# State-space scan: the two differences of the three-part split of B and C on GpSimd instead of VectorE

## The reference, cut to what matters

```python
A = -jnp.exp(A_log)
x_dbl = jnp.einsum('bld,ed->ble', hidden_states, W_xproj)
dt_low = x_dbl[..., :DT_RANK]
Bm = x_dbl[..., DT_RANK:DT_RANK + D_STATE]
Cm = x_dbl[..., DT_RANK + D_STATE:]
delta = jax.nn.softplus(jnp.einsum('blr,dr->bld', dt_low, W_dt) + b_dt)
dA = jnp.exp(delta[..., None] * A)
dBx = (delta * x)[..., None] * Bm[:, :, None, :]
# per token: h = dA_t * h + dBx_t ; y = sum over n of h * C_t
```

## Time and profile before

| | |
|---|---|
| median of 3 runs | 1409.5 us (1409.46 to 1409.54) |
| the profiled execution | 1409.21 us, its span 1407.4 us |
| mean granted TensorE clock over the span | 0.928 |
| TensorE (matmul) busy | 1095.6 us, 78% |
| VectorE busy | 1001.4 us, 71% |
| ScalarE busy | 750.5 us, 53% |
| GpSimd busy | 792.1 us, 56% |

### The profile page before, as it was taken

One profiled execution on the slowest core, in us unless ns is written; L12 is line 12 of the kernel. 1 busy time (PEld: TensorE's weight loads), 2 busy tenths in 40 slices (PEclk: granted clock), 3 DMA queues, 4 the chain that ended last, 5 costly groups with the idle time before them and its releaser, 6 DMA issues. The chain is left out here.

```text
span 1407.4 us, 25930 instructions
## 1 busy us (share of the span) xinstructions
PE 1095.6 (78%) x8527; PEld 755.7 (54%) x8527; DVE 1001.4 (71%) x1898; ACT 750.5 (53%) x1601; POOL 792.1 (56%) x730
## 2 busy tenths in 40 slices
PE   5877778687777757888888888413999999999980
PEld 1332223232232326666666676302898999899970
DVE  2999999999999965777677677484455555555533
ACT  4667575666656624666556565202455555555433
POOL 2686776767777645666677666312234634463423
PEclk8999999999999988999999999556899999999995
DMA  3000000000000000111111110202234443443217
GB/s 106 16 15 1 16 0 15 1 15 15 0 0 0 1 21 13 40 41 34 34 34 34 35 40 25 83 0 93 69 60 111 89 101 73 112 87 73 41 22 252
DMA packets 43463, 64.01 MB, mean 45 GB/s; under 512 B 8288, under 2 KB 34592, under 8 KB 41248
## 3 DMA queue, kind: packets, MB, share of 16 engines
q1 hardware_dynamic: 31104, 46.11, 9.8%
q0 software_dynamic: 12288, 17.05, 7.5%
HBM read 42.00 MB, written 21.14 MB: 45 GB/s over the span
## 5 line engine op out<-in xcount | busy, mean ns | idle before, releaser
L514 POOL TENSOR_TENSOR scan_hc<-scan_state,scan_c_sb 128x1024 f32<-128x1024 f32 x128 | 304.4, 2383 | 143.0 <-DVE scan_state L442 133.6
L442 DVE TENSOR_TENSOR_SCAN scan_state<-scan_decay,scan_drive_ps 128x512 f32<-128x512 f32 x256 | 297.4, 1203 | 0.2
L223 PE MATMUL scan_y_ps<-scan_hc,all_ident 128*128 128x512 f32 x520 | 255.3, 614 | 2.1 <-POOL scan_hc L514 2.1
L1660 DVE TENSOR_TENSOR expert_hid_lo<-expert_hid,expert_hid_hi 128x512 fp32r<-128x512 f32 x128 | 88.6, 692 | 176.0 <-ACT expert_hid_hi L1644 176.0
L1557 POOL DMA_INDIRECT acc<-expert_rows,expert_lst x64 | 112.0, 1750 | 180.4 <-DVE expert_rows L1686 165.7
L1639 ACT ACTIVATE expert_hid<-expert_h_ps,expert_b 128x512 f32<-128x512 f32 x128 | 88.2, 689 | 199.2 <-PE expert_h_ps L556 199.2
L435 DVE TENSOR_TENSOR scan_drive_ps<-scan_dx,scan_b_ps 128x512 f32<-128x512 f32 x256 | 162.6, 681 | 14.9 <-POOL scan_dx L501 10.8
L326 ACT ACTIVATE scan_decay<-scan_delta,scan_a_neg 128x508 f32<-128x508 f32 x256 | 169.2, 715 | 7.4 <-POOL scan_delta L496 7.2
L368 ACT ACTIVATE scan_c_sb<-scan_c_ps 128x512 f32<-128x512 f32 x128 | 76.6, 598 | 138.0 <-PE scan_c_ps L216 128.9
L556 PE MATMUL expert_o_ps<-weights_w_hi,expert_hid_lo 128*128 128x256 f32 x512 | 143.3, 280 | 0.0
L554 PE MATMUL expert_o_ps<-weights_w_hi,expert_hid_hi 128*128 128x256 f32 x512 | 143.3, 280 | 0.0
(11 more groups left out here) (221 smaller groups left out, 2498.3 us busy)
## 6 DMA issues: line engine op xcount, KB each, us to landing
weights_w<-w SPq DMA_DIRECT2D x16, 1024.0 KB, 5.3
table<-all_row SPq DMA_DIRECT2D x32, 132.0 KB, 1.7
scan_xT<-xT SPq DMA_DIRECT2D x8, 512.0 KB, 3.9
attn_ctxT<-ctxT SPq DMA_DIRECT2D x32, 128.0 KB, 2.5
acc<-all_row SPq DMA_DIRECT2D x32, 128.0 KB, 1.7
final_a<-acc SPq DMA_DIRECT2D x8, 512.0 KB, 6.5
out<-final_o SPq DMA_DIRECT2D x8, 512.0 KB, 4.6
expert_b<-b SPq DMA_DIRECT2D x8, 128.0 KB, 2.9
```

Of the source, the lines that this page charges most:

```text
L223: last = pe.matmul(y_ps[k][:], ident[0][:], hc[:, n % RING, k, :], start=False, stop=(n == NS - 1))
L442: dve.tensor_tensor_scan(state[:, n % RING, k, :], decay[:, n % RING, k, :, :].rearrange("p b t -> p (b t)"), drive_ps[k][:], 0.0, ALU.mul ...
L514: pool.tensor_tensor(hc[:, n % RING, :, :], state[:, n % RING, :, :], c_sb[:, n % RING, :].unsqueeze(1).broadcast_to([P, KH, GT]), ALU.mul ...
L1660: dve.tensor_tensor(hid_lo[:, f % RING_H, :], hid[:, f % 2, :], hid_hi[:, f % RING_H, :].bitcast(F32), ALU.subtract).then_inc(hid_ready, 1)
```

## The change

Both differences go to GpSimd, and since it reads SBUF, ScalarE makes one more copy of the value, in f32, for it (`bc_full`, 64 rows). The parts stand in the opposite order: the last part in rows 0 to 31 of `bcs`, the middle in 32 to 63, the high part stays in 64 to 95. `bc_rest` has 64 rows instead of 96. ScalarE's middle part moves from behind step 9 to behind step 10, ahead of the softplus. TensorE's `step_size` waits for the copy (`bc_copied`) instead of for the difference, and the first broadcast of a group waits on `bc_step` instead of on `bcs_ready`.

```diff
@@ TensorE
                     pe.wait_ge(dt_copied, g + 1)
-                    pe.wait_ge(bc_high, g + 1)
-                    pe.wait_ge(bc_step, 4 * g + 1)
+                    pe.wait_ge(bc_copied, g + 1)
...
-                        pe.wait_ge(bcs_ready, g + 1)
+                        pe.wait_ge(bc_step, 4 * (g + 1))
@@ ScalarE
                     act.activation(bcs[par][:], m_ps[1][0:96, :], ACT.Copy).then_inc(bc_high, 1)
+                    if not first:
+                        act.wait_ge(bc_step, 4 * (g - 1) + 1)
+                    act.activation(bc_full[:], m_ps[1][0:64, :], ACT.Copy).then_inc(bc_copied, 1)
...
                     act.activation(bcs[par][32:64, :], bc_rest[32:64, :], ACT.Copy).then_inc(bc_step, 1)
-                    act.activation(bc_mid[64:96, :], bc_rest[64:96, :], ACT.Copy).then_inc(bc_step, 1)
+                    act.activation(bc_mid[:], bc_rest[0:32, :], ACT.Copy).then_inc(bc_step, 1)
...
-                            if n == 9:
+                            if n == 10:
                                 middle_part(i + par, 1 - par)
-                            if n == 10:
                                 softplus_parts(g + 1)
@@ VectorE
-                def split(i, par):
-
-                    g = 2 * i + par
-                    dve.wait_ge(bc_high, g + 1)
-                    dve.tensor_tensor(bc_rest[:], m_ps[1][0:96, :], bcs[par][:], ALU.subtract).then_inc(bc_step, 1)
-
-                def last_part(i, par):
-                    g = 2 * i + par
-                    dve.wait_ge(bc_step, 4 * g + 3)
-                    dve.tensor_tensor(bcs[par][64:96, :], bc_rest[64:96, :], bc_mid[64:96, :], ALU.subtract).then_inc(bc_step, 1)
-                    dve.wait_ge(bc_step, 4 * g + 4)
-                    dve.sem_inc(bcs_ready, 1)
@@ GpSimd
+                def rest_part(i, par):
+                    g = 2 * i + par
+                    pool.wait_ge(bc_high, g + 1)
+                    pool.wait_ge(bc_copied, g + 1)
+                    pool.tensor_tensor(bc_rest[:], bc_full[:], bcs[par][0:64, :], ALU.subtract).then_inc(bc_step, 1)
+
+                def last_part(i, par):
+                    g = 2 * i + par
+                    pool.wait_ge(bc_step, 4 * g + 3)
+                    pool.tensor_tensor(bcs[par][0:32, :], bc_rest[0:32, :], bc_mid[:], ALU.subtract).then_inc(bc_step, 1)
...
                         if not final:
+                            if n == 8:
+                                rest_part(i + par, 1 - par)
+                            if n == 10:
+                                last_part(i + par, 1 - par)
```

More of the change, by code:

```diff
@@ L93, in scan_phase @@
         bcs = [s.sb(f"bcs{i}", [96, GT], BF16) for i in range(2)]
-        bc_rest = s.sb("bc_rest", [96, GT])
-        bc_mid = s.sb("bc_mid", [96, GT], BF16)
+        bc_full = s.sb("bc_full", [64, GT])
+        bc_rest = s.sb("bc_rest", [64, GT])
+        bc_mid = s.sb("bc_mid", [32, GT], BF16)
         dt_low = s.sb("dt_low", [R, GT])
@@ L131, in scan_phase @@
         bc_step = s.sem("bc_step")
-        bcs_ready = s.sem("bcs_ready")
+        bc_copied = s.sem("bc_copied")
         z_ready = s.sem("z_ready")
@@ L465, in group @@
                             statistics(g)
-                        if n == 8 and not final:
-                            split(i + par, 1 - par)
-                        if n == 10 and not final:
-                            last_part(i + par, 1 - par)
                 dve.sem_inc(drive_ready, 1)
@@ L474, in _ @@
                 dve.memset(eps[:], EPS).then_inc(zeroed, 1)
-                split(0, 0)
                 dve.wait_ge(a_ready, 1)
                 dve.tensor_scalar(a_neg[:], a_exp[:], -1.0, None, ALU.mult).then_inc(a_ready, 1)
-                last_part(0, 0)
                 with dve.Fori(0, GROUPS // 2 - 1) as i:
@@ L534, in _ @@
                 pool.sem_inc(hc_ready, RING)
+                rest_part(0, 0)
+                last_part(0, 0)
                 step_sizes(0, 0, first=True)
```

## The result

The changed kernel takes 1391.71 us in the median of 4 runs (1389.68 to 1396.12), against 1409.48 us (1407.28 to 1409.54) for the kernel before: ratio 0.9873, 95% interval 0.9853 to 0.9892. A second set of runs on another occasion gave 0.9880 (0.9858 to 0.9902). So it is faster by 1.2 to 1.3%. The forecast was 1391.8 us. That the median lies 0.1 us from it is luck: the four runs spread over 6.4 us, and on the second occasion the medians differ by 16.8 us instead of 17.8.

The account below looks back on a forecast made before the run. VectorE's queue was taken to bound the scan. Seven groups at 3.38 - 0.85 = 2.53 us give 17.7 us off 1409.2, so 1391.5, plus 0.3 for the median: 1391.8 us; 8-in-10 range 1386 to 1398.

Parts of the forecast that it names:

- The ceiling, 3.38 us per group: VectorE's queue: removing both differences frees 2.31 and 1.05 us, 3.38 us per group, at most 23.7 us in seven.
- 0.85 us stay as a wait for TensorE: Drive of step 9: the broadcast of B behind TensorE's projection comes late, so 0.85 us per group remain as a wait.
- Rival A: Step 9: TensorE isn't in the way and all 23.7 us come back, 1385.8 us; chance 0.12.
- 2.53 us per group, 17.7 in all: Whole scan: 3.38 less 0.85 us saved in each of seven groups, 17.7 us less in all.
- GpSimd's price: Each difference on GpSimd costs 1.28 us, at most 2.38, and nothing on VectorE, with 1.8 us of slack at the chain's end.
- Rivals C: GpSimd's mixed small differences are far dearer: gain gone at 4.6 us each, 1423 us at 5.5; chance 0.04.
- D: GpSimd's time is on the path: both differences paid in full, 17.9 us against 17.7 saved, 1409.4 us; chance 0.03.
- TensorE's clock: Granted clock in the scan: less TensorE idle time makes it no worse there; 2 us allowed for it.
- the four rivals: Rival A, Rivals C and D, and one with ScalarE's reordering or GpSimd's backlog closer than counted, 1400 us, chance 0.11.
- ScalarE at nothing: ScalarE, steps 9 to 13: the added copy and moved middle copies cost nothing, covered by 1.7 us of slack.
- Start-up at nothing: Preparation for group 0: the new copy and differences fall in GpSimd's idle time before the first delta, costing zero.
- The shared interface: VectorE instructions contend with GpSimd's SBUF reads only with two SBUF inputs, so the new differences slow VectorE by zero.

Follow-up runs that it names:

- e6: The changed kernel with TensorE's projection and its z matmuls both cut in two, half of the latter behind step 11's B broadcast: 1387.45 us, ratio 0.9848.
- e5: The changed kernel with TensorE's projection cut in two, its B and C rows moved behind the broadcast of B for step 9: 1386.77 us, ratio 0.9845.
- e1: The changed kernel with the first difference back on VectorE and only the last on GpSimd, middle part behind step 9: 1401.40 us, ratio 0.9946.
- e2: The changed kernel with the last difference back on VectorE, on partitions 0 to 31, and only the first on GpSimd: 1393.90 us, ratio 0.9895.
- e3: The changed kernel with useless arithmetic of 512 elements on 64 partitions ahead of each GpSimd difference: 1389.78 us, ratio 0.9864.
- e4: The changed kernel with useless arithmetic of 1536 elements on 64 partitions ahead of each GpSimd difference: 1397.78 us, ratio 0.9919.
- e8: The changed kernel with ScalarE's middle part moved back behind step 9: 1390.06 us in one run.
- e0: Both kernels run and profiled again without edits: 1407.35 us for the kernel before, 1391.48 us for the changed one, ratio 0.9880.
- e9: The kernel of e6 with the wait of e7 added: 1385.97 us, ratio 0.9839.
- e7: The changed kernel with VectorE's preparation of the attention's weights waiting for GpSimd's last product of the scan: 1391.64 us, ratio 0.9860.

## Why the prediction was right, point by point

**The ceiling, 3.38 us per group.** The removed part is 2.31 + 1.05 us, and both were the change's. Together with 0.15 us at step 11, which the prediction left out (it counted only to the drive of step 11, and the 3.57 us of that step came from the same instruction), it is 3.5; the undisturbed group of e6, 56.57 us against 60.11, shows as much. A small term was missing, not a wrong step.

**0.85 us stay as a wait for TensorE.** The mechanism was right, the size 0.08 us short. The prediction counted from start to start of the drives, and so counted the step as 0.85 us longer; it is 4.35 - 3.42 = 0.93. The 0.85 us in the profile's brackets are idle time, another quantity, and their agreement is chance. The term that was short is the one from the end of the broadcast to the drive: 0.07 us, taken from ScalarE, against 0.15 on VectorE. e5 shows that it is the broadcast behind the projection. Rival A, all 23.7 us, fell by this; had the term been left out, the forecast would have been some 6 us too low.

**2.53 us per group, 17.7 in all.** Measured 1.38 + 1.05 + 0.15 = 2.58 per group, 18.1 in seven, and 18.3 to 18.4 over the scan. The two slips, 0.08 us too much and 0.15 too little, nearly cancel, which is luck. The remaining 0.2 us are step 0 of the first group (3.44 instead of 3.57) and step 8 of the last preparing group (4.24 us). e1 and e2 show that the terms stand by themselves: 8.4 us for the last difference alone; for the first alone 4.35 us at step 8, as with both.

**GpSimd's price, taken as 1.28 us, covered up to 2.38.** Measured 1.16 and 1.15; e3 with 2.2 costs nothing. The chain went as counted: product 11 starts at 127.02, 12.1 us behind the point from which the prediction counts (111.49 + 3.42 = 114.91; forecast 12.0), and product 13 ends at 138.6, which is 23.7. e4 puts the slack at the full clock at 2.0 us, against 1.8. Rivals C and D would have needed 4.6 us per difference, or no slack.

**TensorE's clock, "no worse there".** This step was wrong, and cost nothing. The product of step 13 now keeps TensorE waiting for 0.5 to 1.0 us ahead of its sum, where it didn't wait before, and in 1 and 2 of 7 groups the sum then took 3.3 to 3.7 us instead of 1.98. The slack of 1.8 us, counted at the full clock, just covers that; e3 shows nothing left of it, and in e4 and e6 the waits of VectorE come or grow with it. None of the four rivals had this. The mean granted clock over the span stayed the same, 0.927 and 0.930 against 0.928 and 0.931.

**ScalarE at nothing.** Right: steps 9 to 13 are 3.42 to 3.44 us with the new copy, and e8 shows the same for the move. Copy 11 ended at 126.79, 11.9 us on the same scale, forecast 12.0.

**Start-up at nothing.** Right by e0, though the first two profiles differed by 2.93 us there. From those alone the prediction would have seemed 3 us off in one place, with 2.5 us of it taken back by the late end.

**The shared interface.** Taking two SBUF inputs off VectorE gave product 10 its 0.49 us back: it takes 2.36 us in e1 too, where only the last difference moved, and 2.72 in e2, where that one is on VectorE. The new differences slow no drive or scan (1.27 and 2.33 us beside them). As the prediction put the other half, that a VectorE instruction with at most one SBUF input does not contend, it is too wide: the casts at the end of the scan have one, and they and the product hold each other up.

## What to carry to other kernels

When a wait is removed, look in the same queue order for the wait it was covering; here it was 0.93 of 3.5 us, and reading it off gave the scan's gain to within 1 us. Work can be moved to an engine that is busy for 70% of the time if it falls into that engine's pauses, and the test is the end of the chain behind it, counted in us, since e3 cost nothing and e4 6 us. Count that chain at the engine's lower clock too, if it can fall there: 1.7 of the 1.8 us of slack went that way. A comparison of two single profiles needs a second one of each: the start of the scan moved by 2.3 us and its end by 2.5 us between executions of one and the same kernel.

## What the runs showed of the hardware

- A difference on GpSimd of 512 elements a partition, f32 and bf16 mixed, took 1.16 us on 64 partitions with f32 output and 1.15 on 32 with bf16 output; two f32 inputs on 128 partitions took 1.276.
- The same small difference on VectorE cost 1.20 us of its time on partitions 64 to 95 with a wait for its landing, and 0.60 us on partitions 0 to 31 without (e2).
- VectorE's casts from SBUF to SBUF and GpSimd's product hold each other up: 0.69 or 2.83 us for the same cast, 3.31 or 2.38 for the product. The cast ahead and the product started 0.22 us apart in both cases, so the start times in the profile don't tell which one loses.
- TensorE's sum of four matmuls took 1.98 us at the full clock and up to 3.68 at the lower one, its broadcasts 0.38 and 0.63. The idle time directly ahead of the sum of product 13 didn't decide which: after 2.0 to 2.2 us of it the clock was low in 8 of 13 groups (e4, e6, e9), after 0.84 to 0.89 in all seven of e3, after 0.5 to 1.0 in 1, 2, 4 and 6 of 7 in four profiles (the changed kernel twice, e7, e8), and with 0.03 or less in none of 21 (the kernel before twice, e2). What does decide is not shown.
